# How far GpSimd's row gathers run ahead of TensorE in two mixture-of-experts stages: 4 tiles, changed to 8

## The reference, cut to what matters

```
scores = softmax(x @ wt.T + g @ wg.T ...)            # 8 experts
topk_w, topk_idx = top_k(scores, 2)                  # 2 experts for each token
gp = leaky(einsum('th,ehm->etm', x, w_gate)); up = einsum('th,ehm->etm', x, w_up)
y_all = einsum('etm,emh->eth', gp * up, w_down)
y = (y_all[topk_idx, tokens] * topk_w).sum(1)  +  shared expert p
```

## Time and profile before

| | |
|---|---|
| median of three runs | 2563.11 us (2559.32 to 2566.83) |
| profiled execution, its own time | 2563.11 us |
| its span in the trace | 2561.2 us |
| PE / DVE / ACT / POOL busy | 93% / 53% / 43% / 42% |
| first layer's gathers, L3004 | 39, from 971.1 to 1031.9 us |
| second layer's gathers, L4199 | 46, from 2298.7 to 2404.3 us |
| DMAs from POOL's queue (software_dynamic) | 20.06 MB, 2.8% of the DMA engines' time |

### The profile page before, as it was taken

The page is one execution under the profiler, slowest core; times in us unless marked ns, Lnnn a source line. Parts: engine busy times, 40 slices in busy tenths (PEclk is TensorE's granted clock), DMA queues, the critical chain, the costliest instruction groups (busy, mean ns, idle before and its releaser), DMA issues. The chain is left out here.

```text
span 2561.2 us, 38155 instructions
## 1 busy us (share of the span) xinstructions
PE 2372.1 (93%) x13184; PEld 1535.7 (60%) x13184; DVE 1358.2 (53%) x3191; ACT 1092.2 (43%) x2686; POOL 1075.3 (42%) x1117
## 2 busy tenths in 40 slices
PE   7999999899999989889999999999999989978865
PEld 4565656543434357678786868656565566656644
DVE  7575665467677544342333333456556467834464
ACT  4767586445545413311112111166657625524322
POOL 3655465258777615452121212366556320014420
PEclk9999999989999989999999999999999999989987
DMA  5000000000000043520000010233324200053311
GB/s 166 1 1 1 1 1 22 5 13 13 13 11 11 6 131 114 181 82 1 1 1 1 1 44 1 67 121 113 104 83 129 72 1 1 1 178 108 113 32 38
DMA packets 101614, 127.02 MB, mean 50 GB/s; under 512 B 17842, under 2 KB 80123, under 8 KB 101044
## 3 DMA queue, kind: packets, MB, share of 16 engines
q1 hardware_dynamic: 94116, 104.52, 13.0%
q0 software_dynamic: 7312, 20.06, 2.8%
HBM read 102.87 MB, written 17.47 MB: 47 GB/s over the span
## 5 line engine op out<-in xcount | busy, mean ns | idle before, releaser
L1005 POOL TENSOR_TENSOR cb_sc<-cb_toep,cb_mk 128x128 f32<-128x128 f32 (+3 forms) x256 | 215.9, 873 | 190.5 <-ACT cb_pr L1043 179.8
L1005 POOL TENSOR_TENSOR cb_bias<-cb_bias,cb_mk 128x128 f32<-128x128 f32 (+3 forms) x256 | 215.3, 873 | 146.6 <-DMA cb_bias<-in_fside_16xSxS 146.4
L1639 DVE TENSOR_REDUCE gb_bmax<-PS 128x8 f32<-128x512 f32 x256 | 164.5, 685 | 87.0 <-PE PS L1417 86.6
L389 PE MATMUL PS<-ident,cb_pr 128*128 128x128 f32 x1280 | 198.8, 285 | 4.0 <-ACT cb_pr L1043 2.3
L690 DVE CUSTOM_DVE_ANT_0 cb_sc<-PS,cb_sc,cb_sneg 128x128 f32<-128x128 f32 (+3 forms) x256 | 129.9, 547 | 125.0 <-PE PS L379 121.4
L389 PEld LDWEIGHTS PS<-ident,cb_pr 128*128 128x128 f32 x1280 | 135.3, 141 | 97.1 <-issue 82.8
L1798 ACT ACTIVATE gb_pt<-PS 128x512 f32<-128x512 f32 x256 | 139.4, 596 | 110.9 <-PE PS L1424 105.7
L1049 ACT ACTIVATE cb_pt<-PS 128x128 f32<-128x128 f32 (+3 forms) x448 | 163.7, 414 | 39.0 <-PE PS L389 38.6
L1417 PE MATMUL PS<-gb_ks,gb_qs 32*128 32x512 f32 x512 | 171.6, 669 | 8.0 <-DVE gb_bmax L1639 6.4
L690 DVE CUSTOM_DVE_ANT_0 cb_bias<-PS,cb_bias,cb_sneg 128x128 f32<-128x128 f32 (+3 forms) x256 | 129.3, 546 | 90.2 <-PE PS L379 89.2
L2322 PE MATMUL PS<-eb_g,ff_h 128*128 128x256 f32 x768 | 173.6, 379 | 0.0
(11 more groups left out here) (713 smaller groups left out, 4996.1 us busy)
## 6 DMA issues: line engine op xcount, KB each, us to landing
cb_bias<-in_fside_16xSxS SPq DMA_DIRECT2D x64, 256.0 KB, 2.9
cb_bias<-in_fside_16xSxS SPq DMA_DIRECT2D x64, 192.0 KB, 2.5
ff_h<-in_L_ffn_h_w SPq DMA_DIRECT2D x2, 4096.0 KB, 15.8
cb_bias<-in_fside_16xSxS SPq DMA_DIRECT2D x64, 128.0 KB, 2.3
y_group<-eb_ys SPq DMA_DIRECT2D x22, 256.0 KB
y_rows<-eb_g SPq DMA_DIRECT2D x19, 256.0 KB
cb_toep<-rel_table SPq DMA_DIRECT2D x8, 512.0 KB, 7.8
x_rows<-X SPq DMA_DIRECT2D x2, 2048.0 KB, 8.5
```

The lines of the kernel that those rows point to most:

```text
L389: ins = pe.transpose(PS[:, bank, j * P:j * P + P], pr[:, v % 2, e, j * P:j * P + P], ident)
L1005: ins = pool.tensor_tensor(biases(v, e), turned(h, n) if L0 else biases(v, e), mk[:, b % 2, packed(t):packed(t) + n], ALU.add)
L1639: dve.tensor_reduce(bmax[:, n % 2, t, g + e, 0:NB], PS[:, bank + e, :].rearrange("p (n k) -> p n k", k=64), AX.X, ALU.max)\
```

## The change

The constant `AHEAD` = 4 is taken out, and the depth `XG` = 8 of the buffer stands in its place. Gather k now waits only for the turn of tile k - 8. In the second layer the written order of POOL's queue changes as well: 8 gathers of the second group stand ahead of the first 4 rows back, and 2 behind them, where 4 and 6 stood.

```
-AHEAD = 4
...
                 for k in range(TILES):
-                    if k >= AHEAD:
-                        pair_x.wait_filled(pool, ("x", (k - AHEAD) // 2))
+                    if k >= XG:
+                        pair_x.wait_filled(pool, ("x", (k - XG) // 2))
                     pool.indirect_dma_start(xg[:, k % XG, :], None, x_rows,
...
                         k = grp * GT + t
-                        if k >= AHEAD:
-                            before_it = k - AHEAD
+                        if k >= XG:
+                            before_it = k - XG
                             pair_x.wait_filled(pool, (before_it // GT, before_it % GT // 2))
...
                 routing.wait_emptied(pool, ("rows", 1))
-                gather(1, range(AHEAD))
+                gather(1, range(XG))
                 pool.wait_ge(sm["mo_slots"], 2)
                 stored(0)
                 return_rows(0, range(0, 4))
-                gather(1, range(AHEAD, 10))
+                gather(1, range(XG, 10))
                 return_rows(0, range(4, 8))
                 gather(1, range(10, 14))
```

## The result

The changed kernel takes 2581.86 us (median of 6 runs, 2575.68 to 2593.18) against 2563.57 for the one before on the same chip (6 runs, 2554.13 to 2569.34). The ratio is 1.0079, 95% interval 1.0058 to 1.0099: slower by 18 us by the medians (20 by the ratio) where +8.5 was forecast. The ratios here are the record's own and need not be the quotients of the medians beside them (they differ by up to 0.0014), and two executions on chip 2 at a granted clock of 0.67 and 0.20 (3302 us for before, 10825 us for e5) are left out of them. The profiled execution took 2579.63 us, with a span of 2577.7.

A forecast was written before the change was run, and what follows sets the result against it. The prediction took PE, busy 93% of the span, to bound the kernel. Its terms, 3.9 + 4.6 + 0 = +8.5 us, gave 2571.6 us, with an 8-in-10 range of 2557 to 2583 us.

The forecast's parts named there:

- That an unbroken run of POOL's indirect DMAs holds PE's news: Both layers: during long POOL runs, word that PE's matmuls are done reaches other engines late; forecast +8.5 us, chance 0.47.
- more than about five: POOL's queue: the length of an unbroken run of indirect DMAs above which PE's news was taken to be late.
- 2.5 us: Release of PE's late news: assumed to come about 2.5 us after the POOL run's last issue.
- the first rival: Both layers: nothing is held, only PE's waits for gathers go, at most 3.3 us, giving 2559.8 us; chance 0.29.
- The start of the first layer, +3.9: First layer's first pairs: a run of ten gathers delays news of PE's second turn; fifth pair 3.9 us later.
- The start of the second layer, +4.6: Second layer's first group: a run of ten gathers makes PE's second turn reported 4.6 us later.
- The second group, 0: Second layer's second group: a longer first hold offset by a shorter later one; 0, bounds +5.2 to -9.2 us.
- The rest of the way, nothing: Behind both layers' tiles: no term given; the work there follows one after the other, so delays pass on.
- The sum: Whole kernel: 3.9 + 4.6 + 0 = +8.5 us, so 2571.6 us.
- Only the waits for gathers go (0.29): Both layers: PE loses only its gather waits, at most 3.3 us, giving 2559.8 us, no change; chance 0.29.
- The second group gains, the starts don't lose (0.10): First layer -1.5 us, second layer's second group -9.2 as its jam breaks, giving 2552.4 us; chance 0.10.
- More is lost (0.14): Both starts get second holds and slow clock, second group +5.2 with nothing won back: 2585.8 us; chance 0.14.

The follow-up runs named there:

- e5: Lookahead of six in both layers, against the kernel before with four: 2545.83 us, ratio 0.9980.
- e1b: Lookahead of eight in the first layer only, four kept in the second, against the kernel before, on a holding chip: 2570.55 us, ratio 1.0023.
- e2b: Lookahead of eight in the second layer only, four kept in the first, against the kernel before, on a holding chip: 2572.92 us, ratio 1.0027.
- e7: Changed kernel plus a short POOL pause after every two indirect DMAs, gathers and rows back; against the kernel before 2555.53 us, ratio 0.9963.
- e6: Kernel before (lookahead four) plus a POOL pause after every four indirect DMAs, gathers and rows back: 2561.29 us, ratio 0.9998.
- e11: Changed kernel (lookahead eight) plus POOL pauses after every four indirect DMAs; against the kernel before 2565.89 us, ratio 1.0002.
- e2: Lookahead of eight in the second layer only, four kept in the first, against the kernel before, on a non-holding chip: 2541.43 us, ratio 0.9969.
- e1: Lookahead of eight in the first layer only, four kept in the second, against the kernel before, on a non-holding chip: 2546.87 us, ratio 0.9994.

## Why the prediction was wrong, and where it was right

*That an unbroken run of POOL's indirect DMAs holds PE's news*, and so the sign: right on chips 1 and 3, and by its parts (e1b, e2b) on chip 4. It was read from the earlier trace rows alone, and the recorded updates and the gaps of e7 bear it out. The sign is in part luck: the same reading gives the wrong one on chips 2 and 6. Its "more than about five" is too high, since runs of four with gaps still hold (e6, e11), and its 2.5 us is too small for a run of fourteen or sixteen (3.2 to 3.8 in the tiles). The Trainium skill's rule in "SBUF — State Buffer", "Who interferes with whom", that DMA never contends with a compute engine, agrees with the trace as far as the matmuls go: eight of them take 1.99 us beside the gathers both on chip 1 (981.24) and on chip 6 (979.12). What suffers is the handing on of their end, which the rule doesn't speak of. On chips 2 and 6 the first rival, which the prediction put beside it, would have given the right sign.

*The start of the first layer, +3.9.* This step failed, by its size. It took the news of PE's second turn to be late, so that POOL would stop after ten. But that turn was handed on at once (ended 980.32, update 980.37, copy 980.39) and the third's in the middle of the run (copy at 984.64), so that POOL was let on to fourteen, and what was held was the end of the second pair's matmuls. The run was four gathers longer (5.0 us), and the release came 3.35 us behind its last issue (3.17 to 3.54 at the layers' starts in the other runs), for 2.5 assumed. The fifth pair's matmuls begin at 998.53, not 996.2. Measured in the tiles: +6.4.

*The start of the second layer, +4.6.* The same error: fourteen, release after 3.27 us, and the first group's last L3267 (L3266 after) ends 63.8 us behind the layer's first gather in place of 57.6: +6.2.

*The second group, 0.* About right: the tiles of both groups together are 7.3 us late, so the group itself adds some 1.1. But the way was another: the run was of sixteen, with a stall of PE of 9.62 us, and about as much was won back.

*The rest of the way, nothing.* The prediction put no term there, and 3.4 us are lost: from the last tile of the first layer to the second layer +2.2 (8.6 - 6.4), behind the second layer's tiles +1.2 (8.5 - 7.3). It is PE's own work that got longer, by 4.0 and 2.3 us of busy time for the same matmuls. In the second stretch its granted clock is 0.75 in place of 0.78; in the first it rounds to 0.98 both times. The time at the lower clock there is 51.2 us for 44.4, and 69.8 for 61.0 in the second. Whether the holds cause this, or it differs so between any two executions, isn't shown.

*The sum.* 6.4 + 6.2 + 1.1 + 3.4 less the start's 0.6 is the 16.5 us of the two spans, where 3.9 + 4.6 + 0 + 0 was forecast: the two starts miss by 4.1 us together, the second group by 1.1, the rest by 3.4.

*Only the waits for gathers go (0.29).* False on chip 1. On chips 2 and 6 nothing is held, and its sign is right (e2 and the changed kernel), but its price of 3.3 us is too small: 9.7 us measured on chip 6, interval 6 to 13. PE waits for gathers for 5.5 us in the second layer with lead four on chip 2 (e1) and 2.2 with lead eight on chip 6, and the second layer's tiles are 2 to 6 us shorter (119.1 against 117.0 and 113.3). The trace thus accounts for only a part of the 9.7. It may be that rows from a chip that holds underrate these waits, since there PE is itself kept back.

*The second group gains, the starts don't lose (0.10).* False on chip 1: both starts lose, 6.4 and 6.2 us, and the second group gains nothing.

*More is lost (0.14).* Its 2585.8 us were nearer to the result than the forecast, but not for its reason: POOL, once released, didn't issue more than two in a row in the first layer (from 990.89 on). In the second group it did, sixteen, yet the group's own loss was 1.1 us and not 5.2.

Open: what in a chip or a session makes it hold. The traces show no difference in the issue of the gathers (0.95 + 0.30 us each on both kinds), but one in the landings recorded (the table above). Whether runs of DMAs from SP's queue would hold too wasn't tried.

## What to carry to other kernels

When POOL issues indirect DMAs, don't take it that an earlier issue is free: look whether an unbroken run delays PE's updates. Where it does, a gap after every two (0.8 us were enough), at a pace no slower than the consumer's, ended the delay, and a lead of eight then gained 0.4%; gaps at the rows back alone, with the old lead, gained as much. Where it doesn't, the gaps cost 0.2%. Copies that start late, with releasers that make no sense ("remote", a DMA long done), up to 3.8 us after POOL's last issue, are the mark to look for. A change worth under 1% that touches such runs must be timed in more than one session and on more than one chip: this one is 0.8% slower on one and 0.4% faster on another, and no single chip would have told it.

## What the runs showed that I had not expected

- The same program fell into two kinds in six sessions: the kernel before takes 2563.6 to 2566.1 us in four and 2549.5 and 2550.2 in two, and only in traces of the former is PE's news held.
- A hold has a direction: during it ACT's news reaches PE at once (copy ended 985.24, matmuls at 985.48), while PE's of 983.23 takes 7 us to reach ACT. No recorded update of ACT, DVE or POOL is more than 0.03 us behind its instruction, in any trace. PE's held updates come through in their order, in a burst (990.29 to 990.49).
- The bytes of the run's last gathers don't matter: with 32 KB a gather in place of 128 KB for the last six of a run of fourteen, ACT idled 7.41 us, against 7.17 and 7.85 with full rows.
- A gain may be bought with a pause: filling a tile with zeros for 0.54 us after every two DMAs made the program 9.5 us faster on chip 4, and 5 us slower on chip 6.
